# Multi-query attention in one pipeline over 128 heads instead of one sequence per batch

## The reference, cut to what matters

```python
B, S, _ = x.shape                  # 8, 512, 128
H, Dh = (NUM_HEADS, HEAD_DIM)      # 16 query heads of 8, one key and one value head
Q = (x @ Wq + bq).reshape(B, S, H, Dh).transpose(0, 2, 1, 3)
K = x @ Wk + bk
V = x @ Wv + bv
A = jnp.einsum('bhqd,bkd->bhqk', Q, K)
A = jnp.where(causal, A, -jnp.inf)
P = jax.nn.softmax(A / np.sqrt(Dh).astype(np.float32), axis=-1)
O = jnp.einsum('bhqk,bkd->bhqd', P, V)
return O.transpose(0, 2, 1, 3).reshape(B, S, H * Dh) @ Wo + bo
...
x = x + _layernorm(_L0_attn_ref(_layernorm(x, axis=-1), ...), axis=-1)
```

## Time and profile before

| | us |
|---|---|
| median of 3 runs | 3750.49 |
| lowest, highest | 3749.16, 3756.89 |
| profiled execution: span of its instructions | 3742.5 |
| median less that span | 8.0 |

### The profile page before, as it was taken

The page is one execution under the profiler, slowest core; times in us unless marked ns, Lnnn a source line. Parts: engine busy times, 40 slices in busy tenths (PEclk is TensorE's granted clock), DMA queues, the critical chain, the costliest instruction groups (busy, mean ns, idle before and its releaser), DMA issues. The chain is left out here.

```text
span 3742.5 us, 161624 instructions
## 1 busy us (share of the span) xinstructions
PE 3489.5 (93%) x67234; PEld 2872.1 (77%) x67234; DVE 3020.8 (81%) x4301; ACT 2705.2 (72%) x4147; POOL 2398.5 (64%) x2884
## 2 busy tenths in 40 slices
PE   6999996699999999999999999999999999999995
PEld 3656554588888888888888888888888888888884
DVE  4556554688889888898888888888888889888884
ACT  2444443478887888878888888888788887878873
POOL 1011011677777777777777777777777777777773
PEclk9999998899999999999999999999999999999997
DMA  1000000132222322222322223222232222222222
GB/s 55 4 3 6 3 3 12 48 90 69 70 70 66 90 69 70 70 61 72 92 71 69 67 69 90 70 69 71 66 90 71 69 70 60 72 66 71 69 65 65
DMA packets 161717, 227.93 MB, mean 61 GB/s; under 512 B 42258, under 2 KB 60632, under 8 KB 161496
## 3 DMA queue, kind: packets, MB, share of 16 engines
q1 hardware_dynamic: 161624, 226.85, 24.2%
HBM read 21.00 MB, written 4.19 MB: 7 GB/s over the span
## 5 line engine op out<-in xcount | busy, mean ns | idle before, releaser
L1184 POOL TENSOR_TENSOR by_cos<-by_cos,by_sin 128x1024 f32<-128x1024 f32 x384 | 910.7, 2382 | 13.6 <-DVE by_sin L1538 13.6
L1190 POOL TENSOR_TENSOR by_cos<-by_cos,norms 128x1024 f32<-128x1024 f32 x384 | 733.5, 1910 | 13.0
L1536 DVE TENSOR_TENSOR by_cos<-proj,turns 128x1024 f32<-128x1024 f32 x384 | 470.2, 1225 | 181.7 <-ACT squares L1426 163.0
L1270 PE MATMUL proj<-qkv_hi,xs_hib 128*128 128x512 f32 x1152 | 512.4, 445 | 49.2 <-DVE by_sin L1538 40.2
L1538 DVE TENSOR_TENSOR by_sin<-proj,turns 128x1024 f32<-128x1024 f32 x384 | 466.3, 1214 | 1.4 <-issue 1.4
L1542 DVE TENSOR_REDUCE sumsb<-squares 128x16 f32<-128x1024 f32 x384 | 464.5, 1210 | 1.5 <-DVE w_lo L1605 1.5
L1272 PE MATMUL proj<-qkv_hi,xs_lob 128*128 128x512 f32 x1152 | 458.3, 398 | 0.0
L1271 PE MATMUL proj<-qkv_lo,xs_hib 128*128 128x512 f32 x1152 | 458.2, 398 | 0.0
L1426 ACT ACTIVATE squares<-proj 128x1024 f32<-128x1024 f32 x384 | 392.7, 1023 | 85.1 <-PE proj L1272 84.7
L1279 PE MATMUL ring<-ident,by_cos 128*128 128x128 f32 x3072 | 385.3, 273 | 8.4 <-DVE xT L1639 5.5
L1406 ACT ACTIVATE vb<-proj 128x1024 f32<-128x1024 f32 x192 | 195.5, 1018 | 255.6 <-DMA v_win<-vb 237.7
(11 more groups left out here) (175 smaller groups left out, 8182.1 us busy)
## 6 DMA issues: line engine op xcount, KB each, us to landing
v_win<-vb SPq DMA_DIRECT2D x1152, 128.0 KB, 2.4
v_win<-vb SPq DMA_DIRECT2D x768, 64.0 KB, 2.0
in_qkv<-L_ffn_Wqkv SPq DMA_DIRECT2D x12, 768.0 KB
wo<-L_ffn_Wo SPq DMA_DIRECT2D x6, 512.0 KB, 4.0
x_tok<-L_attn_x SPq DMA_DIRECT2D x8, 256.0 KB, 4.6
residual<-x_tok SPq DMA_DIRECT2D x8, 256.0 KB, 2.0
o_x<-residual SPq DMA_DIRECT2D x1, 2048.0 KB, 7.7
out<-o_x SPq DMA_DIRECT2D x8, 256.0 KB, 2.3
```

The source lines that it names most:

```text
L1184: nc.gpsimd.tensor_tensor(both, both, by_sin[:, j, :], ALU.add).then_inc(e[f"{w_}_added"].sem, 1)
L1190: nc.gpsimd.tensor_tensor(heads, heads, inverse, ALU.mult).then_inc(e[f"{w_}_ready"].sem, 1)
L1270: nc.tensor.matmul(out, xs_hi[:, tile], qkv_hi[:, cols], start=True, stop=False)
L1536: nc.vector.tensor_tensor(of_heads(by_cos[:, t % 2, j, :]), heads, table(0), ALU.mult)
```

## The change

`mqa_stage` becomes one list of 176 steps on every engine (`steps`), one for each of the 128 heads and some before and behind. The step n does T of head n and S of head n + 6, whatever batch these are in. All the other work of a batch is hung on a fixed head number `h` of the batch before it or of one or two batches behind it. The parts:

- No `Fori` and no `first` or `last` copies: the eight batches are straight code, and all waits are on constants. Queries, values and keys have two buffers, by the batch's parity.
- S of two heads makes 5 fills in place of 8 (`fills`): query tile 3 alone (512 columns); tile 2 beside tile 0 (384 + 128), with one mask of 256; tile 1 of both heads (256 + 256), with one mask. The maxima are 7 `tensor_reduce` for a pair in place of 8. The three fills of an even head and the two of an odd one stand between its T's.
- V of a group is one run of 16 matmuls at `h % 4 == 1` of the next group.
- The bias of a projection is one broadcast matmul for the whole bank, in place of one per tile.
- The layer norms are applied on GpSimd (12 `tensor_scalar` of 128x128 a batch), the residual sum too. ScalarE copies the projected output to `o` first, and VectorE takes its statistics from there. The statistics of all eight inputs are taken ahead of the first head, seven of them in two lumps before the first maxima.
- The keys are copied once by ScalarE (`k_flat`) and spread by four `tensor_scalar` of 128x512 on GpSimd (`spread_keys`), in place of four copies on ScalarE and VectorE and the 128x2048 one on GpSimd.
- `constants_stage` is gone: its work is in the same block, and the first input is loaded first. The mask of the transposed scores stays a matmul.

```diff
+AHEAD = 6
 SLOTS = 32
-AHEAD = 5
...
+def steps():
+
+    for n in range(FIRST_STEP, LAST_STEP):
+        yield n, n // MQA_H, n % MQA_H
+
+
+def batch_of(b):
+    return 0 <= b < B
+
+
+def fills(m):
+
+    if not 0 <= m < HEADS:
+        return ()
+    first = PAIR_FILLS * (m // 2)
+    return ((3, first), (2, first + 1), (1, first + 2)) if m % 2 == 0 else ((3, first + 3), (2, first + 4))
...
+            def normal_output(b, tiles):
+                pool.wait_ge(rstd_done[1], b + 1)
+                for t in tiles:
+                    last = normal_tile(1, b, o[:, t, :], o[:, t, :], t)
+                    if t == TILES - 1:
+                        last.then_inc(o_done, 1)
...
+            def spread_keys(b, i):
+
+                pool.wait_ge(k_flat_done, b + 1)
+                at_least(pool, st_full, 3 * MQA_H * (b - 1))
+                nc.gpsimd.tensor_scalar(kT[b % 2][:, i, :], k_flat[:, :], own_rows[:, i:i + 1], None,
+                                        ALU.mult).then_inc(keys_done, 1)
...
-            def scores(b, g, i, qt):
-
-                s = (g * PER_GROUP + i) * TILES + qt
-                n = P * (qt + 1)
-                out = score[s % 2]
-                pe.wait_ge(e["s_max"].sem, e["s_max"].at(s - 1, b))
-                nc.tensor.matmul(out[:, 0:n], qT0[:, g, qt * P:(qt + 1) * P], kT[:, i, 0:n], start=True, stop=False)
-                nc.tensor.matmul(out[:, n - P:n], ident_bf[:, :], c["mask_qk"][:, :],
-                                 start=False, stop=True).then_inc(e["s_full"].sem, 1)
...
+            def scores(m, qt, fill):
+
+                b, g, i = m // MQA_H, m % MQA_H // PER_GROUP, m % PER_GROUP
+                out, keys = score[fill % 2], kT[b % 2]
+                at_least(pe, s_max, fill - 1)
+                queries = lambda k: qT0[:, g, k * P:(k + 1) * P]
+                if qt == 3:
+                    if i % 2 == 0:
+                        pe.wait_ge(q_done, GROUPS * b + g + 1)
+                        pe.wait_ge(keys_done, PER_GROUP * b + i + 2)
+                    nc.tensor.matmul(out[:, :], queries(3), keys[:, i, :], start=True, stop=True,
+                                     skip_group_check=True)
+                    masked, mask = out[:, 3 * P:4 * P], mask_qk[:, 0, :]
+                elif qt == 2:
+                    nc.tensor.matmul(out[:, 0:3 * P], queries(2), keys[:, i, 0:3 * P], start=True, stop=True,
+                                     skip_group_check=True)
+                    nc.tensor.matmul(out[:, 3 * P:4 * P], queries(0), keys[:, i, 0:P], start=False, stop=True,
+                                     skip_group_check=True)
+                    masked, mask = out[:, 2 * P:4 * P], mask_qk[:, :, :]
+                else:
+                    swapped = keys[:, i + 1, 0:2 * P].rearrange("p (t n) -> p t n", n=P)[:, ::-1, :]
+                    nc.tensor.matmul(out[:, 0:2 * P], queries(1), keys[:, i, 0:2 * P], start=True, stop=True,
+                                     skip_group_check=True)
+                    nc.tensor.matmul(out[:, 2 * P:4 * P], queries(1), swapped, start=False, stop=True,
+                                     skip_group_check=True)
+                    masked, mask = out[:, P:3 * P], mask_qk[:, :, :]
+                nc.tensor.matmul(masked, ident_bf[:, :], mask, start=False, stop=True,
+                                 skip_group_check=True).then_inc(s_full, 1)
...
-                pe.wait_ge(e["q_first"].sem, e["q_first"].at(1, b + 1))
-                head(b, for_max=(b + 1, 0, 0), weighted=(GROUPS - 1, (0, 1)))
-                turn_values(b, GROUPS - 2)
-                head(b, for_max=(b + 1, 0, 1), weighted=(GROUPS - 1, (2, 3)), between=lambda: turn_queries(b, 1))
-                head(b, for_max=(b + 1, 0, 2), between=lambda: turn_queries(b, 2))
-                turn_values(b, GROUPS - 1)
-                head(b, for_max=(b + 1, 0, 3))
-                turn_attn(b)
-                turn_queries(b, 3)
-                project_out(b)
-                head(b, for_max=(b + 1, 1, 0), between=lambda: turn_first(b))
...
+                ahead = fills(n + AHEAD)
+                for k in range(3):
+                    if 0 <= n < HEADS:
+                        scoresT(n, k)
+                    if k < len(ahead):
+                        scores(n + AHEAD, *ahead[k])
+                group = n // PER_GROUP - 1
+                new, old, older = b + 1, b - 1, b - 2
+                if h % PER_GROUP == 1 and 0 <= group < B * GROUPS:
+                    weighted_values(group)
+                elif h % PER_GROUP == 2:
+                    if 0 <= group + 2 < B * GROUPS:
+                        turn_with_max(group + 2)
+                    if 0 <= group < B * GROUPS:
+                        turn_values(group)
+                if batch_of(new):
+                    if h == 3:
+                        turn_xn(new)
+                    elif h in (4, 5):
+                        project(new, h - 4)
+                    elif h == 7:
+                        turn_keys(new)
+                    elif h in (8, 9):
+                        turn_queries(new, h - 8)
+                    elif h in (11, 12):
+                        turn_queries(new, h - 9)
+                if batch_of(old):
+                    if h == 7:
+                        turn_attn(old)
+                    elif h == 8:
+                        project_out(old)
+                if batch_of(older) and h == 13:
+                    turn_y(older)
...
+            def input_statistics(b):
+                dve.wait_ge(x_loaded[min(b, 1)], 16 * (B - 1) if b else 16)
...
+            for n, b, h in steps():
+                if n == FIRST_STEP:
+                    input_statistics(0)
+                    other_constants()
+                    dve.wait_ge(padded, 1)
+                elif -MQA_H + 6 <= n < -MQA_H + 8:
+                    for later in (range(1, B // 2) if n == -MQA_H + 6 else range(B // 2, B)):
+                        input_statistics(later)
+                for fill in fills(n + AHEAD):
+                    maxima(n + AHEAD, *fill)
+                group = n // PER_GROUP - 1
+                new, old, older = b + 1, b - 1, b - 2
+                if h % PER_GROUP == 1 and 0 <= (n + AHEAD) // PER_GROUP < B * GROUPS:
+                    negated_maxima((n + AHEAD) // PER_GROUP)
```

953 lines of the change are left out of this document (426 added, 527 removed).

## The result

The changed kernel takes 3585.68 us in the median of four runs (3582.8 to 3586.76), the kernel before 3753.69 us (3749.16 to 3762.15): a ratio of 0.9554, 95% interval [0.9538, 0.9569]. The forecast was 3665, with a range from 3635 to 3710. The direction and the mechanism held, but the gain is 168 us where 85 were forecast.

A forecast was written before the change was run, and what follows sets the result against it. TensorE was taken as the bound, with about 12.6 us of waits a period. Start 45 + 7 x 61.8 + last batch 49.8 + tail 24.8 = 552.2 us stage end, span 3657, plus 8.0 gives 3665 us; range 3635 to 3710.

The forecast's parts named there:

- The skeleton: Attention stage as start, seven periods, last batch and tail, with the layers behind it shifted unchanged; stage end 552.2 us.
- the period: One batch in steady state: 57.8 us of TensorE work plus 4 of waits, 61.8 us, between 58.8 and 67.5.
- T and S, 37.1: TensorE's score matmuls of a batch: 16 heads at 2.32 us, taken as unchanged by the merged fills.
- Waits, 4: TensorE waiting for the two score banks: 4 us a batch, between 1 and 9.7; the seam's 5.4 go.
- Projections, 5.3: TensorE's projections of a batch: output projection 2.5 us in place of 3.23, two input projections 2.8 in place of 3.2.
- The last batch: Batch 7 to the end of T: 61.8 us less six heads' S and the next batch's projection and turns, 49.8.
- The start: Up to head 0's T: first maximum at about 32 us behind VectorE's statistics, then 13; 45 us, between 42 and 48.
- The tail: Behind the last T: 22.8 us before plus 2 for norms and sum on GpSimd and the copy to `o`, 24.8.
- The 8.0 us around the span: Distance of the median time above the profiled span, added to a span of 3657 us to give 3665.
- The banks hold: Rival: VectorE's delays at the score banks show in full, period 67.5 to 71 us, 3690 to 3739 us; 15%.
- The code is slow to fetch: Rival: TensorE stands for instruction fetches of the straight code, 8 us a batch, 64 in all, 3729 us; 5%.
- The clock: Rival: TensorE's clock falls to its lower level, up to 3920 us; 4% with similar waits; 0.99 or more expected.

The follow-up runs named there:

- the run with split values: Changed kernel with a group's weighted values in three pieces between the T and S pieces of the head, not one run behind them: 3602.0 us, ratio 0.9601.
- the run with fills between: Changed kernel with eight single fills for two heads, each head beginning with a fill (S T S T S T S): 3633.0 us, ratio 0.9687.
- the single fills: Changed kernel with one fill per query tile again, eight fills and masks for two heads in place of five: 3670.5 us, ratio 0.9779.
- all four edits undone: Changed kernel with single fills, drain between batches, values in three pieces and a bias matmul per tile, all together: 3780.1 us, ratio 1.0078.
- my drain: Changed kernel with the first six heads' 15 fills and their maxima in one piece ahead of each batch's first T: 3639.4 us, ratio 0.9699.

## Why the prediction was wrong

**The skeleton held.** The layers moved as they were, the seam vanished, TensorE is the bound, VectorE is busy for 34 us of a batch, and no maximum is slower beside GpSimd's work (means of 687, 556 and 280 ns against 687, 555 and 286). GpSimd works 20.9 us a batch, not 17, and it is hidden.

**The step that failed is the period: 57.8 of work and 4 of waits, measured 52.9 and 0.9.** The time fell in the end below 3638, which I had given 6%. By the period's terms, for a batch:

- *T and S, 37.1, measured 33.0.* "2.32 us for T and S of one head" was taken as the head less its piece of V. But V starts 0.16 us behind the mask ahead of it where a score matmul would start 0.04 behind, in the run with split values and in this very head of the kernel before (its V is at 229.00, the mask in the row below). These 0.12 us belong to V, and without them the head is 2.20, as the run with fills between shows it bare. The other 0.13 is the merging, which I had put at "3 x 0.04 cheaper or as much dearer" for a pair. Together 16 x 0.25 = 4.0 us. The same mistake set the lower end of the range: the work had no lower bound.

```profile
228.84 0.23 PE L311 MATMUL a_score<-mask_qk,ident_bf 128*128 128x128 bf16 x1
```

- *Waits, 4, measured under 1.* I scaled the waits among the heads before by the number of hand-overs, 7.2 us for eight against some 4 for five. What decides is how much work stands between a fill and the next fill of its bank, against the fill, its maximum and the hand-over: 1.15 us for tile 2. With merged fills this passes in each plain head; with single fills, two of them back to back, it fails by 0.36. The 7.2 us were not far off for the form that has them: the single fills give 6.5. That their time, 3670, is near my 3665 is chance.
- *Projections, 5.3, measured 4.4.* The wide bias matmul was inside its bounds.
- *Turns, 5.8, measured 6.3,* and V in one run 9.2 for 9.6: small, and of both signs. What V in one run is worth against pieces, 2.5 us a batch, I had only by their sum.

Together that is 8.05 us a period and 56.4 in seven; the first is shorter by 5.9 more for want of a batch before it, an effect I left out, and the second by 0.5: 62.7 us. **The last batch** is 6.3 shorter for the same reasons.

**The start** was 3.9 us too long: VectorE's first maximum is at 29.75 and not 32, and the 15 fills take 11.4 us, not 13. That its statistics hold it is shown (3.45 us come back without them). **The tail** was 1.5 too short. Four normal tiles on GpSimd take 3.13 us where I gave "1.2 to 1.9" by the selects and adds of the earlier trace rows, and there are two such norms in the tail:

```profile
468.67 3.13 POOL L229 TENSOR_SCALAR a_ob<-a_ob,a_stat,a_rstdb 128x128 f32<-128x128 f32 x4
471.89 1.26 POOL L250 TENSOR_TENSOR x_tok<-x_tok,a_ob 128x512 f32<-128x512 f32 x1
474.75 1.03 POOL L225 TENSOR_TENSOR a_rstdb<-a_varb,minus_half 128x4 f32<-128x4 f32 x1 [1.60 <-DVE a_varb L642]
475.88 3.13 POOL L229 TENSOR_SCALAR a_yb<-x_tok,a_stat,a_rstdb 128x128 f32<-128x128 f32 x4
```

By the rule of two that I cited (the Trainium skill, "GPSIMD Engine Reference", section 4.1 "Engine selection") a tile would be 0.68 us, as an estimate; it is 0.78. The section has the two for two-input operations and puts one-input ones at roughly VectorE's rate; this one, with one tensor and two scalars per partition, is far from that rate here.

**The 8.0 us around the span** were no constant: the same kernel has 1.8 us between the span of a run and its time (3586.76 for 3585.0). By that distance the profiled execution of before was a quick one, and I laid its distance to the median on the forecast: 7.3 us.

**The rivals.** *The banks hold:* not in this kernel, but the mechanism is real; it is what two single fills in a row, or 0.7 us more on VectorE before a release, bring back. *The code is slow to fetch:* the instruction queues move 119 packets and 1.42 MB in the whole program, and TensorE, busy for 53.55 of 53.75 us, has no gaps for it. The two cache lines that the Trainium skill gives ("Advanced Engine Details and Errata", section "ISA Cache") have no effect on the period that these runs show; the same section gives TensorE 128 KB in place of 32, which I left out. *The clock:* 1.00 here; with all four edits undone it takes some 6 to 7 us of a period, by the estimate above.

**Where the gain came from,** by undoing one thing at a time, in us of a period: merged fills 8.65 (2.1 of work, 6.5 of waits), no seam 6.3, one wide bias 2.0 and some 0.8 by the clock, values in one run 2.5. These four add up to 20 us where a period fell by 18.6 (72.3 to 53.75); the norms' place gives 1 more. So the sum is no exact account: the parts cover one another a little, and the seam's share is that of my drain and not of the seam before (by the prediction's working, 5.4 us of waits). Why the clock falls where it does is not settled: I see it behind waits and behind narrow matmuls, but no run separates the two.

## What to carry to other kernels

For a pair of banks between two engines, compare the work that stands between a fill and the next fill of its bank with the round trip (fill, reader, hand-over), head by head; neither the reader's busy share nor the count of hand-overs tells whether it waits, and a reordering alone can be worth half of it. Take "packed" work from a stretch that neither begins nor ends at another kind of matmul, and measure waits by distances between starts, because modelled ends hide part of them. When an operation moves to an engine with room, ask first what is queued behind it there: the mask on GpSimd gave nothing until an input norm was asked for six heads earlier, and then 19.5 us.
